# First self-attention: the band is accumulated into the scores by TensorE instead of being subtracted by VectorE

## The reference, cut to what matters

```python
qkv = x @ in_proj_weight.T + in_proj_bias
rel = pos[:, None] - pos[None, :]
bias = jnp.minimum(rel[None, :, :] * slopes[:, None, None], MAX_BIAS)     # MAX_BIAS = 8.0
scores = jnp.einsum('bhqd,bhkd->bhqk', q, k) * D ** (-0.5) + bias[None]
probs = jax.nn.softmax(scores, axis=-1)
out = jnp.einsum('bhqk,bhkd->bhqd', probs, v)
```

## Time and profile before

| | before |
|---|---|
| median of 3 runs | 3141.96 us |
| profiled execution, its own time | 3139.22 us |
| span of the profile | 3137.4 us |
| granted TensorE clock, mean | 0.960 |
| PE / DVE / ACT / POOL busy | 89% / 59% / 42% / 53% |
| the stage of the change, first to last exponential | 162.1 to 470.4 us |

### The profile page before, as it was taken

The page is one execution under the profiler, slowest core; times in us unless marked ns, Lnnn a source line. Parts: engine busy times, 40 slices in busy tenths (PEclk is TensorE's granted clock), DMA queues, the critical chain, the costliest instruction groups (busy, mean ns, idle before and its releaser), DMA issues. The chain is left out here.

```text
span 3137.4 us, 38375 instructions
## 1 busy us (share of the span) xinstructions
PE 2805.0 (89%) x12634; PEld 1764.7 (56%) x12634; DVE 1855.2 (59%) x3754; ACT 1302.2 (42%) x2326; POOL 1662.9 (53%) x1406
## 2 busy tenths in 40 slices
PE   5688886999999999587999999999999999999979
PEld 5344445555565665454656556665656556556557
DVE  2466766665767665446555556556556555556456
ACT  1155564444455455122444444444444444444410
POOL 2144403665666667502466666666666666666710
PEclk8789998999999999797999999999999999999979
DMA  8655613232332321002223232224222233222110
GB/s 278 132 152 163 157 33 109 64 102 51 103 75 54 97 63 32 34 0 73 60 69 74 53 99 68 52 68 106 53 67 68 54 97 75 57 63 63 32 54 27
DMA packets 114229, 245.51 MB, mean 78 GB/s; under 512 B 16239, under 2 KB 62576, under 8 KB 112881
## 3 DMA queue, kind: packets, MB, share of 16 engines
q1 hardware_dynamic: 107824, 219.52, 27.4%
q0 software_dynamic: 5696, 23.42, 2.7%
q10 hardware_dynamic: 512, 0.13, 0.0%
HBM read 106.98 MB, written 31.80 MB: 44 GB/s over the span
## 5 line engine op out<-in xcount | busy, mean ns | idle before, releaser
L1049 POOL TENSOR_TENSOR ACC<-ACC,PR 128x512 f32<-128x512 f32 (+1 forms) x1056 | 1331.0, 1282 | 456.2 <-ACT PR L1274 448.2
L1274 ACT ACTIVATE PR<-banks 128x512 f32<-128x512 f32 (+1 forms) x832 | 468.8, 597 | 669.2 <-PE banks L1163 668.2
L1335 DVE TENSOR_REDUCE mx<-banks 128x2 f32<-128x800 f32 (+1 forms) x512 | 504.1, 986 | 393.6 <-PE banks L1115 392.0
L1179 PE MATMUL banks<-PR,V 128*64 128x512 f32 (+1 forms) x2496 | 599.1, 604 | 0.0
L1162 PE MATMUL banks<-QA,KA 128*128 128x512 f32 (+1 forms) x1248 | 535.5, 429 | 12.3 <-DMA QB<-ROW 11.5
L1115 PE MATMUL banks<-KH,QZ 128*128 128x400 f32 (+1 forms) x1536 | 480.7, 372 | 41.2 <-DVE mx L1335 20.8
L1163 PE MATMUL banks<-QB,KB 65*128 65x512 f32 (+1 forms) x1248 | 495.2, 397 | 0.0
L1115 PEld LDWEIGHTS banks<-KH,QZ 128*128 128x128 f32 x1536 | 267.9, 189 | 225.6 <-issue 89.7
L1274 ACT ACTIVATE PR<-banks,small 128x512 f32<-128x512 f32 (+1 forms) x416 | 269.4, 687 | 300.3 <-PE banks L1163 290.1
L1332 DVE CUSTOM_DVE_ANT_0 banks<-banks,maskadd 128x400 f32<-128x400 f32 (+1 forms) x512 | 289.2, 588 | 143.6 <-PE banks L1115 136.8
L1303 DVE TENSOR_TENSOR KB<-banks,KH 64x400 fp32r<-64x400 f32 (+1 forms) x384 | 219.4, 571 | 260.0 <-ACT KH L1207 254.5
(11 more groups left out here) (243 smaller groups left out, 2977.4 us busy)
## 6 DMA issues: line engine op xcount, KB each, us to landing
KA<-KH SPq DMA_DIRECT2D x192, 400.5 KB
CX<-ctx_split SPq DMA_DIRECT2D x8, 2403.0 KB, 10.4
WK<-wk_split SPq DMA_DIRECT2D x48, 256.0 KB, 5.7
WV<-wv_split SPq DMA_DIRECT2D x24, 512.0 KB, 3.9
QA<-QZ SPq DMA_DIRECT2D x96, 128.0 KB
QB<-QZ SPq DMA_DIRECT2D x96, 128.0 KB
first<-in_w_in SPq DMA_DIRECT2D x8, 1024.0 KB, 6.2
second<-in_w_out1T SPq DMA_DIRECT2D x8, 1024.0 KB, 8.8
```

The lines of the kernel that those rows point to most:

```text
L1049: pool.tensor_tensor(acc, other, PR[0:r, n % RING, :], ALU.add).then_inc(summed, 1)
L1179: last = pe.matmul(OB[h * DH:(h + 1) * DH, :], V[0:r, g % 4, s, h * DH:(h + 1) * DH], PR[0:r, (n + h) % RING, :], start=(s == 0), stop=(s ...
L1274: act.activation(PR[0:r, n % RING, :], SB[n % 3][0:r, :], ACT.Exp, bias=keybias[0:r, g // pairs, t:t + 1] if masked else 0.0).then_inc(pro ...
L1335: dve.tensor_reduce(mx[:, :, t, c], couples[i % 2 if g == 0 else 0][:, :, 0:w], AX.X, ALU.max).then_inc(mx_done, 1)
```

## The change

The subtraction on VectorE is taken out, with the semaphore `biased` and its count `bands`. VectorE makes a negative identity once (`minus`). On a banded tile TensorE leaves the accumulation open after the score matmul and adds a second matmul, `minus` by the band, of fp32 operands, 128 x 128 by at most 128 columns; `sc_ready` comes from the second one. ScalarE waits for `sc_ready` on every tile.

```diff
--- before.py
+++ after.py
@@ -423,10 +423,6 @@
             _, t, h = tile_of(n)
             return S - 1 - t * P > CLAMP[h % H]
 
-        bands = [0]
-        for n in range(N):
-            bands.append(bands[-1] + banded(n))
-
         def before():
             return [("p", 0, 0), ("p", 0, 1), ("v", 0, 0), ("v", 0, 1), ("p", 0, 2), ("p", 0, 3)]
 
@@ -466,6 +462,7 @@
             whole = sb("whole", [P, 1024])
             high = sb("high", [P, 1024], F32R)
             low = sb("low", [P, 1024], F32R)
+            minus = sb("minus", [P, P])
             rec = self.small[:, 0:GN].rearrange("p (t h) -> p t h", t=NT)
 
             def load_rows(sp):
@@ -481,8 +478,8 @@
 
             with self.stage() as (sem, ctx):
                 scaled, ones_made, x_based = sem("s_scaled"), sem("s_ones"), sem("s_based")
-                sc_ready, biased, probs, used, mx_ready, mx_done = (
-                    sem("s_scores"), sem("s_biased"), sem("s_probs"), sem("s_used"), sem("s_mxready"), sem("s_mxdone"))
+                sc_ready, probs, used, mx_ready, mx_done = (
+                    sem("s_scores"), sem("s_probs"), sem("s_used"), sem("s_mxready"), sem("s_mxdone"))
                 job_ready, job_done, full_ready, hi_ready, lo_ready, row_in = (
                     sem("s_job"), sem("s_jobdone"), sem("s_full"), sem("s_hi"), sem("s_lo"), sem("s_rowin"))
                 o_raised, o_step = sem("s_raised"), sem("s_ostep")
@@ -641,6 +638,7 @@
 
                     for x in before():
                         job(x)
+                    pe.wait_ge(scaled, 1)
                     pe.wait_ge(self.self_in, 16 * 12)
                     pe.wait_ge(ones_made, 2)
                     for m in range(LEAD):
@@ -652,8 +650,12 @@
                             pe.wait_ge(probs, n - 2)
                         if n % GN == 0:
                             pe.wait_ge(row_in, 32 * (g + 1))
-                        pe.matmul(SB[n % 3][:, :], keys(h)[:, t * P:(t + 1) * P], queries(h),
-                                  start=True, stop=True).then_inc(sc_ready, 1)
+                        last = pe.matmul(SB[n % 3][:, :], keys(h)[:, t * P:(t + 1) * P], queries(h), start=True, stop=not banded(n))
+                        if banded(n):
+                            o = t * P + int(CLAMP[h % H])
+                            w = min(P, S - o)
+                            last = pe.matmul(SB[n % 3][:, o:o + w], minus[:, :], self.band[:, h % H, 0:w], start=False, stop=True)
+                        last.then_inc(sc_ready, 1)
                         for x in at(n):
                             job(x)
                         if n + LEAD < N:
@@ -699,7 +701,7 @@
                             act.wait_ge(job_ready, place[("turn", g - 1, 0)] + 1)
                         act.activation(RAISED[:, :], OB[:, :], ACT.Copy).then_inc(o_raised, 1)
 
-                    act.wait_ge(scaled, 2)
+                    act.wait_ge(scaled, 3)
                     for x in before():
                         job(x)
                     job(("row", 0, 0))
@@ -707,10 +709,7 @@
                         g = n // GN
                         if n >= RING:
                             act.wait_ge(used, n // GH - 1)
-                        if banded(n):
-                            act.wait_ge(biased, bands[n + 1])
-                        else:
-                            act.wait_ge(sc_ready, n + 1)
+                        act.wait_ge(sc_ready, n + 1)
                         act.activation(PR[:, n % RING, :], SB[n % 3][:, :], ACT.Exp).then_inc(probs, 1)
                         for x in at(n):
                             job(x)
@@ -768,6 +767,7 @@
                         dve.tensor_tensor(A[:, :, c:c + GH * D].rearrange("p t (h d) -> p t h d", h=GH), o[:, :, :, 0:D],
                                           rec.unsqueeze(3).to_broadcast([P, NT, GH, D]), ALU.mult).then_inc(job_done, 1)
 
+                    dve.tensor_scalar(minus[:, :], ident[:, :], -1.0, None, ALU.mult).then_inc(scaled, 1)
                     dve.tensor_scalar(bcs[:, 0:2], self.bcol[:, 0:2], D ** -0.5, None, ALU.mult).then_inc(scaled, 1)
                     dve.tensor_copy(bcs[:, 2:4], self.bcol[:, 2:4]).then_inc(scaled, 1)
                     for x in before():
@@ -776,12 +776,6 @@
                         maxima(m)
                     for n in range(N):
                         g, t, h = tile_of(n)
-                        if banded(n):
-                            o = t * P + int(CLAMP[h % H])
-                            w = min(P, S - o)
-                            dve.wait_ge(sc_ready, n + 1)
-                            s = SB[n % 3][:, o:o + w]
-                            dve.tensor_tensor(s, s, self.band[:, h % H, 0:w], ALU.subtract).then_inc(biased, 1)
                         for x in at(n):
                             job(x)
                         if n + LEAD < N:
```

## The result

The changed kernel takes 3129.4 us, the median of 7 runs (3121.81 to 3134.93), against 3141.45 for the kernel before: a ratio of 0.9961, 95% interval 0.9948 to 0.9974. It is faster by 12 us, where I had put no change, 7 us slower, and a range that ended at 3131. In another set of runs the ratio was 0.9969 (0.9956 to 0.9982). The profiled execution took 3129.40 us, 9.8 less than that of before. All of it lies in the stage: its exponentials span 298.6 us instead of 308.3, and behind them both programs take 2666 to 2667 us.

A forecast was written before the change was run, and what follows sets the result against it. TensorE was taken to bound the stage's groups without projections, a stalling chain to hurt those with them. Added passes +35.5 less 28.4 us removed gave +7, put at 3148 us; 8 in 10 range 3131 to 3165.

The forecast's parts named there:

- What bounds the stage: Stage of 162 to 470 us: TensorE bounds groups 12 and 13; a stall of about 4 us hurts projection groups.
- wholly beside: Groups 12 and 13: VectorE's subtraction, 5.0 us of group 12, runs beside TensorE, which would not notice its going.
- much faster than 300: Sign on the stage's length, forecast about 315 us: far below 300 would mean VectorE was the bound after all.
- Removed, 28.4 us: Gain from dropping the subtraction: turn 15.3, maximum behind LO 2.1, row 1.5, other gaps 2.5, clock 7 us.
- 4.0 of my 28.4: TensorE's waits filled by added passes: 1.5 us at the row, 2.5 us before the second projection and transposes.
- turn waits: TensorE's waits on RAISED before the turn, 22.5 us in 12 places: 0.6 each would stay, 15.3 us come back.
- VectorE's 45 us: Subtraction on VectorE, 152 times 0.30 us; its removal was to take group 12's VectorE time from 14.6 to 9.5 us.
- 35.5 us, on the path: Cost of 152 band matmuls on TensorE: 304 passes at 0.12 us, 36.5, plus 0.5 for low clock, less 1.5 hidden.
- The clock: Full-speed time lost in groups 1, 4, 5, 8, 9, 10.0 us: 7 would return, between 0 and 14.
- the one at 3131, dense TensorE: Faster rival, chance 0.12: turn waits vanish, clock full in group 0 too, 0.11 a pass; 9 to 12 us gained.
- The halved stalls: Slower rival, chance 0.22: turn still waits about 2 us in five places, clock still falls; +20 us, 3162.
- the pair of 0.38 us: Slower rival, chance 0.13: band matmuls not pipelined, each near 0.38 us; +22 more, up to +29, 3171 us.

The follow-up runs named there:

- LO later alone: Kernel before, with VectorE making LO two tiles later in its list and no band matmul on TensorE: 3122.43 us, ratio 0.9933.
- the second band matmul: Changed kernel with another band matmul, of zero weights, added in each of the 152 tiles: 3153.57 us, ratio 1.0048.
- the useless passes: Kernel before, its subtraction kept, with zero-weight band matmuls added on TensorE: 3149.52 us, ratio 1.0017.

## Why the prediction was wrong

- *What bounds the stage*: right for the groups with projections, where the chain HI, LO, maximum, subtraction, exponential, turn is most of what the subtraction cost (LO later alone wins 18 us in the stage). Wrong for the others: I had the subtraction "wholly beside" TensorE in groups 12 and 13, and without it they are 1.9 and 0.9 us shorter. TensorE is the bound there only once the passes are in: the second band matmul is paid at 0.20 to 0.21 us a tile. Of my signs, a stage "much faster than 300" was to mean that this reading was wrong; 298.6 and 296.7 lie on that edge.
- *Removed, 28.4 us*: 30.0 measured in the stage with the band left out, 36 by the ratio. That the stage comes so near is partly luck. 4.0 of my 28.4 are gaps filled by the added passes, so the removal had only 24.4. Its turn waits give back 17.3 us (22.5 to 5.2), not 15.3; groups 12 and 13 give 2.8, for which I had nothing; and the wait for the row's DMA takes 4.5 (2.7 to 7.2), also in no term.
- *VectorE's 45 us*: its busy time in the stage fell by 28 (213 to 185), and in group 12 to 12.1, not 9.5. A busy time counts stretches in which records overlap once, and nothing in the sum hung on it.
- *The step that failed*: "35.5 us, on the path, since TensorE has no other slack in groups 12, 13 and 2". The addition cost 18 to 20 in the stage, 24 to 26 by the ratios, against 31.5 with the 4.0 of filled gaps taken off. Two things were off. A pass is 0.108 to 0.11 us, not 0.12: 33 instead of 36.5. And 13 to 15 us of the passes by the stage, 7 to 9 by the ratios, cost nothing; the lists show 9.8 us of waits filled, which I had priced apart and left standing, or not priced. I let 12 turns wait 0.6 us each after the change, 7.2 in all, and then laid the passes of tiles 4, 5 and 6, which TensorE issues while ScalarE makes the exponential and RAISED, beside this wait as if they came in sequence; measured, the turn waits 2.0 us in all. Groups 12, 13 and 2 had the slack that I denied: the useless passes on top of the kernel before cost 1.1, 1.9 and 1.1 us there, of 3.5, 3.3 and 1.5. The same holds for the row's maxima, for which I took 1.5 us, and for the row's DMA, which was in no term.
- *By group*: 12 and 13 were to lose 2 to 3 us and lost 0.6 and 1.7; groups 2, 6, 10, 14 were to lose 1.4 each and lost 0.5 to 1.8; groups 1, 4, 5, 8, 9 were to win 0.5 to 2 and won 1.2 to 4.5. The reading of group 12 itself held its refutation: I counted 13 us of work in 17.1, and called the group full.
- *The clock*: I took 7 of 10 us for groups 1, 4, 5, 8 and 9; the clock is 1.00 in all of them, so 10.
- *The rivals*: the one at 3131, dense TensorE, was nearest; I held against it that group 0's low clock starts ahead of the first tile. It does (0.50 just ahead of it, before and after), and group 0 still reads 0.90 and 0.96 in the two profiles of the changed kernel where it was 0.84; the full clock was not needed to reach 3131. Its chance of 0.12 was too low. The halved stalls are excluded by the turn's 2.0 us, the pair of 0.38 us by the pace of 0.68 us a tile.

## What to carry to other kernels

Work that is added to the bounding engine is paid only as far as it does not fall into that engine's waits on others; go through its list and let added work and remaining waits overlap, as one sum for each group, before adding terms. When an engine's wait ends with an operation that stood behind an unrelated one in a third engine's list, try the order of that list first: here two tiles of delay for LO won at least as much as moving 152 operations to another engine. For short matmuls count the weight loads beside the moving columns and take the longer of the two. And test "this engine is full" by taking the other engine's work away as well as by adding to its own: groups 12 and 13 moved under both.

## What was unexpected of the hardware

- 304 useless passes on top of the kernel before cost only 5 us. In the profiled execution groups 12, 13 and 2, at full clock, took them at a third to three quarters of their price, and in groups 4 and 5 the granted clock read 1.00 instead of 0.87 and 0.94; the cause of that clock is not shown.
- A band matmul with 8 moving columns takes as much of TensorE's time as one with 128 (0.69 and 0.68 us a tile), while its records show 0.28 and 0.38 us.
- Loads of 16 weight columns start 0.03 us apart, and the fp32 passes of 128 moving columns that they serve still 0.11.
